# Rotary block of a four-block attention kernel: convolution taps moved from GpSimd to TensorE, and the attention loop regrouped by key chunk

## The reference

```python
q = x @ wq.T + bq
k = (x @ wk.T + bk) * scaling
v = x @ wv.T + bv
lepe = conv_general_dilated(v, lepe_w, (1, 1), padding 2, feature_group_count=C) + lepe_b   # 5 x 5, per channel
qr, kr = theta_shift(q, sin, cos), theta_shift(k, sin, cos)   # x * cos + rotate_every_two(x) * sin
attn = softmax(qr @ kr.T + mask)          # 12 heads of 16, 1024 x 1024, mask differs by head
return (attn @ v + lepe) @ wo.T + bo
```

## Time and profile before

| what | us |
|---|---|
| median of 3 runs (range) | 9167.21 (9151.51 to 9183.75) |
| the profiled execution: its own time | 9149.93 |
| its span, first to last instruction | 9148.2 |
| rotary preparation, first to last `vc` (7 image periods) | 6413.72 to 7068.85 |
| rotary loop | about 7232 to 9143 |

### The profile page before, as it was taken

The page is one execution under the profiler, slowest core; times in us unless marked ns, Lnnn a source line. Parts: engine busy times, 40 slices in busy tenths (PEclk is TensorE's granted clock), DMA queues, the critical chain, the costliest instruction groups (busy, mean ns, idle before and its releaser), DMA issues. The chain is left out here.

```text
span 9148.2 us, 201857 instructions
## 1 busy us (share of the span) xinstructions
PE 7613.5 (83%) x68440; PEld 4576.6 (50%) x68440; DVE 5291.4 (58%) x7803; ACT 4525.4 (49%) x8209; POOL 2586.0 (28%) x2843
## 2 busy tenths in 40 slices
PE   2999899989387878846899898997576699999999
PEld 2555555555155555534555555554232355555555
DVE  3655555555255555544555555554777477777776
ACT  1444444444266565632444444444233377777776
POOL 2343443433111112213434343432546200000000
PEclk7899999999699999967999988999777799999999
DMA  6666666664443333347665767663221344444443
GB/s 160 134 124 134 126 124 129 125 136 90 116 75 77 65 74 69 72 127 133 124 126 114 132 114 132 118 125 73 83 80 55 92 125 113 124 111 125 113 123 81
DMA packets 536713, 999.94 MB, mean 109 GB/s; under 512 B 102129, under 2 KB 303026, under 8 KB 500210
## 3 DMA queue, kind: packets, MB, share of 16 engines
q1 hardware_dynamic: 479346, 900.57, 44.4%
q0 software_dynamic: 56576, 88.90, 6.4%
HBM read 646.02 MB, written 335.81 MB: 107 GB/s over the span
## 5 line engine op out<-in xcount | busy, mean ns | idle before, releaser
L1676 DVE TENSOR_REDUCE a_nmp<-a_S 128x2 f32<-128x1024 f32 x1536 | 1878.3, 1224 | 1370.4 <-PE a_S L1524 1354.9
L1777 ACT ACTIVATE a_PROB<-a_T 128x512 f32<-128x512 f32 x3072 | 1668.1, 595 | 1968.4 <-PE a_T L1503 1956.7
L1373 POOL CAST a_RF<-a_RL 32x512 fp32r<-32x512 f32 x1536 | 1295.1, 843 | 1116.7 <-DVE a_RL L1704 1024.5
L2498 DVE CUSTOM_DVE_ANT_0 a_X<-a_S,a_mask 128x1024 f32<-128x1024 f32 x768 | 909.4, 1222 | 608.1 <-PE a_S L2413 592.8
L2531 ACT ACTIVATE a_PROB<-a_T 128x512 f32<-128x512 f32 x1536 | 918.6, 598 | 438.4 <-PE a_T L2426 428.4
L1499 PE MATMUL a_T<-a_QW,a_KW 64*128 64x512 f32 x3072 | 811.4, 521 | 316.5 <-issue 148.4
L2426 PE MATMUL a_T<-a_ident,a_X 128*128 128x128 f32 x6144 | 994.2, 284 | 31.8 <-DVE a_OSB L2511 16.4
L1499 PEld LDWEIGHTS a_T<-a_QW,a_KW 64*128 64x128 f32 x3072 | 313.5, 193 | 1326.3 <-issue 1323.3
L1537 PE MATMUL a_O<-a_PROB,a_V 128*32 128x512 f32 x6144 | 927.6, 680 | 2.5 <-ACT a_PROB L1777 2.5
L962 DVE CUSTOM_DVE_ANT_0 a_PROB<-a_S,a_mask 128x512 f32<-128x512 f32 x768 | 523.0, 688 | 594.4 <-PE a_PT L799 501.2
L2426 PEld LDWEIGHTS a_T<-a_ident,a_X 128*128 128x128 f32 x6144 | 659.8, 141 | 327.3 <-issue 305.6
(11 more groups left out here) (160 smaller groups left out, 10656.5 us busy)
## 6 DMA issues: line engine op xcount, KB each, us to landing
a_QV<-a_part_rows SPq DMA_DIRECT2D x384, 256.0 KB, 7.1
a_rel_rows<-a_RF SPq DMA_DIRECT2D x96, 1024.0 KB, 9.1
a_K<-part_rows SPq DMA_DIRECT2D x576, 128.0 KB, 3.3
a_X<-xn_scratch SPq DMA_DIRECT2D x72, 768.0 KB, 6.5
stream<-a_Y POOLq DMA_DIRECT2D x288, 192.0 KB, 4.7
a_part_rows<-a_part SPq DMA_DIRECT2D x48, 1024.0 KB, 11.6
a_QV<-a_part_rows SPq DMA_DIRECT2D x384, 128.0 KB, 7.6
a_QV<-a_rel_rows SPq DMA_DIRECT2D x384, 128.0 KB, 6.6
```

Of the source, the lines that this page charges most:

```text
L1373: nc.gpsimd.tensor_copy(dst, src).then_inc(permuted, 1)
L1676: nc.vector.tensor_reduce(nmp[:, qh, c, 2 * pr:2 * pr + 2, kh], S[:, pr], AX.X, ALU.max).then_inc(s_done, 1)
L1777: nc.scalar.activation(PROB[:, s % PRING, 2 * pr + sd], T[:, slot(("st", s, pr, sd))], ACT.Exp).then_inc(t_act, 1)
L2498: nc.vector.tensor_tensor_reduce(out=X[:, v % 2, c, g], in0=S[:, sd].rearrange("p a b -> p (a b)"), in1=mask[:, n % 2, g, c], scale=1.0, s ...
```

## The change

In `prepare_rot`, VectorE does 18 taps instead of 16, GpSimd and ScalarE none. TensorE does the other 7 as new jobs `dg`: a matmul of a diagonal 96 x 96 matrix (the tap's weights) with the shifted image, three float32r products for each tap (high x high, high x rest, rest x high), 21 matmuls of 512 columns in a job, 4 jobs for each image. `dg` stands after the first and the second head group. For it the padded values are copied to a rounded `VPH` (ScalarE) and the rest `VPL` (VectorE), the 28 diagonals are built once on VectorE, and ScalarE writes the bias and the `dg` result to `CV`, to which VectorE then adds its taps. `oc` projects one buffer instead of two. On GpSimd the store and the root follow the six additions.

In `attend_rot` a step is a key chunk for both halves of the queries: two groups of four transposes, `(kc, 0)` and `(kc, 1)`, one for each pair of heads, then scores at `kc` 0, 2, 4, 6, then the outputs of the chunk before, 256 queries at once. Scores at `kc` 0 and the last outputs of the unit before stand ahead of the first transposes. `turn` is split: `sum` picks the 8 columns of sums, VectorE takes 8 reciprocals for each partition and widens them (`invert`), `turn` transposes them back, and VectorE multiplies by the PSUM tile (`divide`), one pair of heads later. ScalarE lowers by halves of 512, with a semaphore for each half. `ORDER` has 21 places, with two pads, which leave a bank unused.

```diff
-
-    ON_POOL = tuple(range(16, TAPS * TAPS))
...
     PIECES = 2 * GROUPS
     ORDER = [("vc", m, t) for m in range(2) for t in range(2)]
-    ORDER += [(n, g, h) for g in range(GROUPS) for h in range(2) for n in ("qk", "qkr")]
+    for g in range(GROUPS):
+        ORDER += [(n, g, h) for h in range(2) for n in ("qk", "qkr")]
...
+                if b:
+                    store(b - 1)
+                if b + 1 < IMAGES:
+                    root(b + 1)
...
+                elif n[0] == "dg":
+                    _, m, t = n
+                    if t == 0:
+                        pe.wait_ge(v_rest, 2 * b + m + 1)
+                    alone(pe)
+                    for j, k in enumerate(ON_PE):
+                        dy, dx = divmod(k, TAPS)
+                        here = slice(dy + 16 * t, dy + 16 * t + 16), slice(dx, dx + SIDE)
+                        for i, src in ((0, VPH), (0, VPL), (1, VPH)):
+                            last = nc.tensor.matmul(T[0:HALF, to], DIAG[:, m, j, i], src[:, m, here[0], here[1]],
+                                                    start=j == 0 and i == 0 and src is VPH,
+                                                    stop=j == len(ON_PE) - 1 and i == 1)
...
-                        for k in range(2):
-                            last = nc.tensor.matmul(T[0:HALF, to], wo[:, k, m * HALF:(m + 1) * HALF],
-                                                    src[:, 1 - s, k, t * BANK:(t + 1) * BANK],
-                                                    start=i + k == 0, stop=i + k == 2)
+                    for k in range(2):
+                        last = nc.tensor.matmul(T[0:HALF, to], wo[:, k, m * HALF:(m + 1) * HALF],
+                                                CV[:, 1 - s, k, t * BANK:(t + 1) * BANK], start=k == 0, stop=k == 1)
...
+            nc.vector.tensor_copy(VPH[:], VP[:, 0]).then_inc(set_up, 1)
+            nc.vector.tensor_copy(VPL[:], VP[:, 0]).then_inc(set_up, 1)
+            nc.vector.tensor_copy(lw_hi[:], lw[:]).then_inc(set_up, 1)
+            eng.wait_ge(set_up, SETUP + 5)
+            nc.vector.tensor_tensor(lw_lo[:], lw[:], lw_hi[:].bitcast(F32), ALU.subtract).then_inc(set_up, 1)
+            eng.wait_ge(set_up, SETUP + 6)
+            alone(eng)
+            for j, k in enumerate(ON_PE):
+                for m in range(2):
+                    for i, part_w in enumerate((lw_hi[:].bitcast(F32), lw_lo[:])):
+                        nc.vector.tensor_scalar(DIAG[:, m, j, i], ident_sb[:], part_w[:, m, k:k + 1], None, ALU.mult
+                                                ).then_inc(set_up, 1)
+            eng.wait_ge(set_up, MADE)
...
+                for m in range(2):
+                    eng.wait_ge(high_padded, 2 * b + m + 1)
+                    need(eng, t_ready, done(b - 1, ("dg", 1, 1), "pe") if b else 0)
+                    alone(eng)
+                    nc.vector.tensor_tensor(VPL[:, m], VP[:, b % 2, m], VPH[:, m].bitcast(F32), ALU.subtract).then_inc(v_rest, 1)
...
+                        dst = CV[:, b % 2, m].rearrange("p (a b) -> p a b", a=SIDE)
+                        if j:
+                            eng.wait_ge(taps, ND * b + 2 * j + m - 1)
+                        nc.vector.scalar_tensor_tensor(out=dst, in0=src, scalar=lw[:, m, k:k + 1], in1=dst,
+                                                       op0=ALU.mult, op1=ALU.add).then_inc(taps, 1)
+                    if j == 4 and b + 1 < IMAGES:
                         variance(b + 1)
                     if j == len(ON_DVE) - 3 and b + 1 < IMAGES:
                         normalise(b + 1)
...
+                for m in range(2):
+                    nc.scalar.copy(VPH[:, m], VP[:, s, m]).then_inc(high_padded, 1)
                 for i in range(PIECES):
                     high(PIECES * b + i)
+                    if i in (1, 3):
+                        m = i // 2
+                        for t in range(2):
+                            act.wait_ge(t_ready, done(b, ("dg", m, t), "pe"))
+                            need(act, t_ready, done(b - 1, ("oc", 1, 1), "pe") if b > 1 else 0)
+                            alone(act)
+                            nc.scalar.activation(CV[:, s, m, t * BANK:(t + 1) * BANK],
+                                                 T[0:HALF, ORDER.index(("dg", m, t)) % RING], ACT.Identity, bias=lb[:, m:m + 1]
+                                                 ).then_inc(t_act, 1)
...
-    RING, PRING = 3, 4
-    STEPS = 2 * CHUNKS
-    SCORES_AT = {1: 0, 5: 1}
-    TAIL = ("turn", "wo")
-    TAIL_AT = {3: "turn", 6: "wo"}
-    ORDER = [n for s in range(STEPS) for n in [("t", s)] + ([TAIL_AT[s]] if s in TAIL_AT else [])]
+    RING, PRING = 3, 3
+    SCORES = ((0, 0), (1, 0), (0, 1), (1, 1))
+    SCORES_AT = {0: SCORES[0], 2: SCORES[1], 4: SCORES[2], 6: SCORES[3]}
+    TAIL = ("sum", "turn", "wo")
+    TAIL_AT = {1: ("sum",), 2: ("turn",), 4: ("wo",), 6: ("pad",), 7: ("pad",)}
+    LOWER_AT = {2: (0, 0), 3: (0, 1), 4: (1, 0), 5: (1, 1), 6: (2, 0), 7: (3, 0)}
+    LOWER_LATE = {0: (2, 1), 1: (3, 1)}
+    ORDER = [n for s in range(CHUNKS) for n in [("t", s, 0), ("t", s, 1)] + list(TAIL_AT.get(s, ()))]
...
-                for g in range(G):
-                    last = nc.tensor.transpose(T[:, slot(("t", s)), P * g:P * g + P], X[:, par, c, g, P * kc:P * kc + P],
-                                               ident_sb[:])
+                for sd in range(2):
+                    for c in range(2):
+                        last = nc.tensor.transpose(T[:, slot(("t", kc, p)), P * (2 * sd + c):P * (2 * sd + c) + P],
+                                                   X[:, par, c, 2 * p + sd, P * kc:P * kc + P], ident_sb[:])
                 last.then_inc(t_ready, 1)
 
...
                 for g in range(G):
-                    last = nc.tensor.matmul(O[Q * g:Q * g + Q, par, P * c:P * c + P], V[:, par, kc, g],
-                                            PROB[:, s % PRING, g], start=kc == 0, stop=kc == CHUNKS - 1)
+                    last = nc.tensor.matmul(O[Q * g:Q * g + Q, par], V[:, par, kc, g], PROB[:, kc % PRING, g],
+                                            start=kc == 0, stop=kc == CHUNKS - 1)
...
-                    last = nc.tensor.matmul(T[:, to, 0:2 * P], turn_sb[:], OSB[:], start=True, stop=True)
+                    for c in range(2):
+                        last = nc.tensor.matmul(T[:, to, G * c:G * c + G], OSB[:, P * c:P * c + P], pick_sb[:],
+                                                start=True, stop=True)
+                elif n == "turn":
+                    pe.wait_ge(widened, u)
+                    alone(pe)
+                    for c in range(2):
+                        last = nc.tensor.matmul(T[:, to, P * c:P * c + P],
+                                                inverse_wide[:, P * c:P * c + P], ident_sb[:],
+                                                start=True, stop=True)
...
+                def others(kc):
+                    if kc in SCORES_AT and not (isinstance(u, int) and u == UNITS - 1):
+                        scores(u + 1, 1 - par, *SCORES_AT[kc], nth)
+                    if kc:
+                        outputs(u, par, kc - 1, mine)
+                    elif not isinstance(u, int) or u:
+                        outputs(u - 1, 1 - par, CHUNKS - 1)
+
+                others(0)
...
+                for kc in range(CHUNKS):
                     for p in range(2):
-                        scores(0, 0, c, p, 1)
...
+                        transposed(u, par, kc, p)
+                    if kc:
+                        others(kc)
+                    if not isinstance(u, int) or u:
+                        for n in TAIL_AT.get(kc, ()):
+                            if n != "pad":
+                                tail(u, par, n)
...
+                nc.vector.reciprocal(inverse[:].rearrange("p c g -> p (c g)"), T[:, slot("sum"), 0:2 * G]).then_inc(t_dve, 1)
+                eng.wait_ge(t_dve, upto(v + 1, "sum", "dve"))
+                nc.vector.tensor_copy(inverse_wide[:].rearrange("p (t x) -> p t x", x=Q), inverse[:].rearrange(
+                    "p c g -> p (c g)").unsqueeze(2).to_broadcast([P, 2 * G, Q])).then_inc(widened, 1)
+
             def divide(v):
-
                 eng.wait_ge(t_ready, upto(v + 1, "turn", "pe"))
-                nc.vector.reciprocal(inverse[:], T[:, slot("turn"), 0:2 * P]).then_inc(inverted, 1)
-                eng.wait_ge(inverted, v + 1)
-                nc.vector.tensor_tensor(OSB[:], OSB[:], inverse[:], ALU.mult).then_inc(t_dve, 1)
-
...
+                nc.vector.tensor_tensor(OSB[:], OSB[:], T[:, slot("turn"), 0:2 * P], ALU.mult).then_inc(t_dve, 1)
...
+                if u + 1 < UNITS:
+                    row_max(u + 1, *SCORES[0])
+                if u:
+                    invert(u - 1)
+                if u + 1 < UNITS:
+                    row_max(u + 1, *SCORES[1])
+                if u:
+                    divide(u - 1)
+                if u + 1 < UNITS:
```

(45 more changed lines are left out.)

198 lines of the change are left out of this document (69 added, 129 removed).

## The result

The changed kernel took 9095.33 us (median of 6, 9081.65 to 9097.88) beside 9163.32 for the kernel before on the same chip: ratio 0.9928 [0.9911, 0.9945], 66 us less. Run again on another chip it took 9105.34 beside 9132.42: 0.9972 [0.9956, 0.9987], 26 us less. Differences from before are taken from the ratio, which is an estimate of its own and not the quotient of the two medians (these lie 68 and 27 us apart); differences from the changed kernel are those of medians. The forecast was 19 less. The profiled execution has a span of 9080.0 us where before had 9148.2.

The account below looks back on a forecast made before the run. TensorE was taken to bound the rotary loop, a chain through the engines the preparation. Preparation -11 and loop with entry -8 gave -19 us: 9148 against the median 9167, range 9000 to 9215.

Parts of the forecast that it names:

- The loop, what is late in its place: Rotary loop: waits on other engines take back most of TensorE's saving; unit 19.57 us from 19.68, 11 us gained.
- 11 less 3 of entry: Rotary loop: 11 us gained over 96 units, less 3 once, as all four scores are lowered before the second transposes.
- The third stall: Rotary loop: TensorE's transposes wait near 0.6 us a unit for ScalarE's exponentials.
- the loop's own 0.14 of gaps: Rotary loop: 0.14 us a unit of gaps, taken from before, added to the 19.4 us schedule to give 19.57.
- What TensorE saves: Rotary loop: if nothing were late, a unit takes 17.0 us, 2.65 less, 255 us in all.
- The preparation: Rotary preparation, a chain through the engines: 8 - 21 - 7 + 9 = -11 us.
- Set-up +9: Before the preparation's images: VectorE's copies, 28 diagonals and weight splitting lie on the path and cost 9 us.
- Last image and `oc` -28: Preparation's last image: `oc` starts 97.3 us after `vc` instead of 118.4, -21; `oc` has 16 records less, -7.
- The periods: Preparation, from one image's `vc` to the next: 94.8 us against 93.6, seven times, +8.
- rival (c): Preparation: float32r matmuls take two passes, +18 us an image, +144, 9290 us; chance 0.07 together with other losses.
- rival (b): Rotary loop: stalls lower TensorE's granted clock to 0.93, costing 131 us, 9280 us; chance 0.13.
- Rival (a), no stalls,: Rotary loop: the stalls, or half of them, don't come; 100 to 255 us gained, 8905 to 9060 us; chance 0.18.

Follow-up runs that it names:

- Experiments 4 to 6: Changed kernel with VectorE's division ahead of the second row maximum (8997.64 us), with the last scores one key chunk earlier (9027.77), and with both (8948.76).
- experiment 6: Changed kernel with both loop edits, division ahead of the second row maximum and last scores one key chunk earlier: 8948.76 us, ratio 0.9802 to before.
- experiment 8: Changed kernel with TensorE's taps reading 512 contiguous columns, shifts left out, so another output; one run: 0.230 us a matmul, periods 95.0 to 96.3.

## Why the prediction was right or wrong

**The loop, what is late in its place: right.** In forecast and trace, from the unit's first transposes: `(2, 0)` at 3.50 and 3.46, scores 1 at 4.60 and 4.46, `(4, 0)` after its stall at 9.0 and 8.89, scores 3 at 14.77 and 14.62 (7698.19 is 5.73 behind 7692.46), scores 0 after theirs at 18.18 and 18.04, the next unit at 19.42 and 19.28. Stalls: 1.1 and 1.04, 0.6 and 0.54. Experiments 4 to 6 take each away by itself, and the unit shortens by 1.11 and 0.60. The third stall, forecast as 0.6 of transposes waiting for exponentials, comes in part, and no list of waits names it. In the records inside the `x16` row the fourth group starts 0.31 behind the last transpose of the third, in each unit, where its neighbours follow at 0.11: 0.20 for the bank, where 0.22 was forecast. Ahead of `(2, 0)` stand 0.23 for ScalarE's copy of `O` in every second unit, and in the others `(2, 0)` starts 0.58 behind `sum` instead of 0.47.

**The loop's size: 41.6 us where 11 less 3 of entry was forecast.** The schedule was 0.14 too long, and the prediction added the loop's own 0.14 of gaps from before on top, which don't show: 0.29 x 96 = 28 us. The entry did cost its 3 us: from the first scores to the first transposes it is 16.53 us (7206.26 to 7222.79), 12.72 before (7232.72 to 7245.44). About 6 us come back at the two ends, which the sum left out. The first unit takes 17.38 us (7222.79 to 7240.17), since it has no division to wait for, and the last has no scores of a next one.

**What TensorE saves: right in kind, half a microsecond a unit too much.** Without the listed waits a unit is 19.28 - 1.7 = 17.6 us (as experiment 6 has, 17.6 with 0.13 of waits), not 17.0, and 0.2 of the difference is the bank above. Outputs of 256 columns start their follower 0.57 later, as said, scores 0.66 too; transposes take 8.2 instead of 7.95 in seven groups, the 0.2 included, `sum` and `turn` 1.1 instead of 0.9, `wo` 0.94 instead of 0.85. It didn't reach the time, because both stalls count from TensorE's scores to VectorE's end: what TensorE does between them is cover.

**The preparation: the term that was mis-sized.** Forecast -11, measured +7.2 with the entry's gap. Set-up +9: from the end of the stage before to the first `vc` 34.5 became 43.1, +8.6. Last image and `oc` -28: from its `vc` to the last matmul 134.2 became 107.4, -26.8. Entry gap +1.5. The periods: 94.8 forecast against 97.0 on average (97.3 steady), +23.9 in place of +8. The mis-sized term is a matmul on the diagonals, 0.213 taken from the scores and 0.248 measured, with 0.65 for the first of each group: two groups of 42 take 10.80 us each (7100.68 to 7111.48) instead of 8.95, +3.7 a period. `vc` to the first tap is 56.9 where 54.2 was said; without the diagonals that is 35.3, 1.0 under the 36.3 on which the forecast built. From there to the next `vc` it is 40.5 where 40.6 was said; taps are 43.13 / 36 = 1.198 throughout. So one float32r pass, as forecast; rival (c), two passes at 0.43, is refuted.

**The clock, rival (b): refuted.** The granted clock in the loop is 1.00 with idles of 1.04 and 0.54 us in each unit. The Trainium skill's rule on short idles between groups that cycle through PSUM banks ("TensorE: Matmul & The Clock Gate", A second HAM failure mode) would have had it swing here; these idles didn't do it.

**Rival (a), no stalls,** is refuted for this kernel by the 96.5 and 49.1 us of waits; experiment 6 makes it by hand: 8949 us, inside its 8905 to 9060. Against the time on record, 9148, the second comparison came out at 9105 and the first at 9095; 15 us of this is the changed stages, and the rest the other stages and the session, which no step priced. That the changed stages came so near is partly luck: the loop gave 34 us more than its 8, the preparation and its entry gap 18 less than its 11, and the two misses stand against each other.

## What to carry to other kernels

When waits are taken away, lay the new order out in time and look for the instruction that now stands behind a long one on another engine: here a 0.41 us division behind 3 us of row maximum cost 105 us of a possible 203, and moving it was worth more than the whole change. Work moved to an idle engine helps only if it runs beside the old work: 7 taps on TensorE ahead of VectorE's gave nothing, behind the value jobs 95 us. And a cover that is priced at nothing has to be priced again at every further step; GpSimd's store and power came due as soon as the period shrank (4.7 us a period), and VectorE as the next bound at 22 taps.

## What the runs showed of the hardware

A float32r matmul of 96 x 96 by 512 columns, each with a weight load, takes 0.230 us with contiguous columns. In rows of 32 out of 36 it takes 0.234 to 0.236 where the rows start at a multiple of four columns, and 0.254 to 0.260 where they don't (experiment 8). TensorE kept its full clock (1.00) in a loop where it is idle 9% of the time, mostly in pieces of 1.04 and 0.54 us, while the relative-position stages, idle 11 to 12%, get 0.89 to 0.91, and one of them differs by 37 us between executions of the same instructions: more than the change's own gain, and seen only because each stage was compared by itself.
